# Layer norm before the experts' routing: half of the groups on ScalarE, and the first expert number read ahead

## The reference, cut to what matters

```python
x = x + retention(_layernorm(x))
x = x + _moe(_layernorm(x), Wg, bg, w1, w2)
x = x + recurrence(_layernorm(x))
x = x + _moe(_layernorm(x), Wg, bg, w1, w2)

def _layernorm(x, axis=-1, eps=1e-05):
    return (x - mean) / sqrt(var + eps)

def _moe(x, Wg, bg, w1, w2):
    logits = t @ Wg.T + bg                      # 4096 x 8
    topw, topi = top_k(softmax(logits), 2)
    # each token goes to its two experts:
    #   gate, up = split(t @ w1e.T); o = (silu(gate) * up) @ w2e.T
    # and the two results are added with normalised weights
```

## Time and profile before

| | us |
|---|---|
| median of 3 runs | 1347.71 |
| lowest and highest | 1342.36, 1349.99 |
| profiled execution, its own time | 1351.96 |
| its span, first to last instruction | 1350.1 |
| TensorE busy | 1148.6 (85%) |
| VectorE busy | 927.6 (69%) |
| ScalarE busy | 612.8 (45%) |
| GpSimd busy | 551.3 (41%) |

### The profile page before, as it was taken

One profiled execution on the slowest core, in us unless ns is written; L12 is line 12 of the kernel. 1 busy time (PEld: TensorE's weight loads), 2 busy tenths in 40 slices (PEclk: granted clock), 3 DMA queues, 4 the chain that ended last, 5 costly groups with the idle time before them and its releaser, 6 DMA issues. The chain is left out here.

```text
span 1350.1 us, 34954 instructions
## 1 busy us (share of the span) xinstructions
PE 1148.6 (85%) x14041; PEld 818.7 (61%) x14041; DVE 927.6 (69%) x1959; ACT 612.8 (45%) x1310; POOL 551.3 (41%) x537
## 2 busy tenths in 40 slices
PE   7999999975699999478999999899987648999970
PEld 4677777763588888235555555555555436888850
DVE  6778787757765655568778797877854376656546
ACT  3344343413355555153736456374653233555534
POOL 3333233202377776325162341516321105777750
PEclk9999999988799999698999999999997679999995
DMA  8132222009643332200000101000000195333338
GB/s 305 55 109 95 88 93 86 35 1 346 209 170 104 104 102 89 72 32 3 33 3 33 33 3 33 4 32 4 2 2 3 33 387 159 104 103 103 105 108 336
DMA packets 50682, 125.66 MB, mean 93 GB/s; under 512 B 7648, under 2 KB 26976, under 8 KB 47712
## 3 DMA queue, kind: packets, MB, share of 16 engines
q1 hardware_dynamic: 36896, 86.20, 17.8%
q0 software_dynamic: 13632, 37.24, 8.8%
HBM read 79.63 MB, written 43.78 MB: 91 GB/s over the span
## 5 line engine op out<-in xcount | busy, mean ns | idle before, releaser
L1090 POOL DMA_INDIRECT ffn_xs<-xn_rows,ffn_from_row x142 | 137.7, 969 | 123.0 <-DVE ffn_second_y_at L1472 80.4
L1098 POOL DMA_INDIRECT y_rows<-ffn_ys,ffn_to_row x142 | 140.2, 987 | 54.9 <-issue 35.2
L1253 PE MATMUL ffn_ps_h<-ffn_w_high,ffn_xst 128*128 x568 | 155.1, 395 | 0.7 <-issue 0.7
L1500 DVE TENSOR_TENSOR ffn_act_in<-ffn_silu_g,ffn_ps_h 128x256 f32<-128x256 f32 x142 | 59.9, 422 | 139.1 <-ACT ffn_silu_g L1132 139.1
L1132 ACT ACTIVATE ffn_silu_g<-ffn_ps_h 128x256 f32<-128x256 f32 x142 | 54.8, 386 | 144.3 <-PE ffn_ps_h L1253 144.3
L1273 PE MATMUL ffn_ps_o<-ffn_w,ffn_act_t 128*128 x284 | 117.2, 435 | 0.5 <-DVE ffn_act_t L1505 0.5
L1253 PEld LDWEIGHTS ffn_ps_h<-ffn_w_high,ffn_xst 128*128 128x128 f32 x568 | 97.3, 190 | 18.2 <-issue 1.2
L1833 POOL TENSOR_TENSOR rec_mixed_w<-rec_mixed_w,rec_xnt 128x512 f32<-128x512 f32 x16 | 17.2, 1090 | 200.0 <-DVE rec_mixed_w L2635 200.0
L1253 PE MATMUL ffn_ps_h<-ffn_w_low,ffn_xst 128*128 x284 | 89.8, 398 | 0.0
L644 DVE TENSOR_TENSOR ret_probs<-ret_score,ret_causal 128x2048 f32<-128x2048 f32 x32 | 73.3, 2292 | 18.2 <-PE ret_score L485 18.2
L1275 PE MATMUL ffn_ps_o<-ffn_w,ffn_act_t 128*128 x284 | 79.2, 279 | 0.0
(11 more groups left out here) (353 smaller groups left out, 2890.2 us busy)
## 6 DMA issues: line engine op xcount, KB each, us to landing
home<-y_rows SPq DMA_DIRECT2D x30, 512.0 KB, 4.8
w_split<-home SPq DMA_DIRECT2D x24, 512.0 KB, 4.3
ffn_w_high<-w_split SPq DMA_DIRECT2D x8, 1024.0 KB, 8.8
ffn_w_low<-w_split SPq DMA_DIRECT2D x8, 1024.0 KB, 10.6
ffn_w<-w_split SPq DMA_DIRECT2D x8, 1024.0 KB, 14.6
home<-in_f_w SPq DMA_DIRECT2D x12, 512.0 KB, 5.8
xn_rows<-home SPq DMA_DIRECT2D x12, 512.0 KB, 11.7
out<-x SPq DMA_DIRECT2D x8, 512.0 KB, 5.7
```

What stands on the lines that cost most here:

```text
L1090: pool.indirect_dma_start(xs[:, n % SLOTS, :], None, xn_rows[:], bass.IndirectOffsetOnAxis(ap=from_row[:, n:n + 1], axis=0)) \
L1098: pool.indirect_dma_start(y_rows[:], bass.IndirectOffsetOnAxis(ap=to_row[:, m:m + 1], axis=0), ys[:, m % SLOTS, :], None).then_inc(ys_stor ...
L1253: mm = pe.matmul(ps_h[:, u % 2, :], one_pass(xst[:, u % 2, part, k, :]), one_pass(w1[w_part][k][:, bass.ds(e, E_COLUMNS)]), start=(part + ...
L1500: dve.tensor_tensor(act_in[:, u % 2, :], silu_g[:, u % 2, :], ps_h[:, u % 2, FF:2 * FF], ALU.mult) \
```

## The change

Two edits. In the norm stage, VectorE norms the even groups as before. The odd groups (1, 3, 5, 7) are normed by ScalarE, as `Identity(x * rstd + offset)`, where `offset` = -mean * rstd is made by VectorE in four small operations, one for each piece of GpSimd's. On ScalarE, group 1 and group 3 come ahead of xnt(0), group 5 ahead of xnt(2), and group 7 ahead of xnt(4). The semaphore `xn_ready` becomes two, one for each engine. In the loop's start, the wait for w1 and the TENSOR_LOAD of the first packed expert numbers come ahead of the transposes of the first two row tiles. The other edits of the diff are a new name (`expert_at` for `offset`) in TensorE's code.

```diff
+        offset = sb("offset", [P, TILES])
...
-        xn_ready = sem("xn_ready")
+        ln_offset = sem("ln_offset")
+        xn_ready = [sem(f"xn_ready{h}") for h in range(2)]
...
-                    sp.wait_ge(xn_ready, n + 1)
+                    sp.wait_ge(xn_ready[n % 2], n // 2 + 1)
...
             @block.scalar
             def _(act):
+                def norm(n):
+                    act.wait_ge(ln_offset, sum(first <= n for first in ROOTS))
+                    for j in range(UNROLL):
+                        i = n * UNROLL + j
+                        op = act.activation(xn_of[n][:, j, :], x[:, i, :], ACT.Identity, bias=offset[:, i:i + 1],
+                                            scale=rstd[:, i:i + 1])
+                    op.then_inc(xn_ready[1], 1)
+
+                norm(1)
                 for n in range(STEPS):
+                    if n % 2 == 0 and n + 3 < STEPS:
+                        norm(n + 3)
                     act.wait_ge(xt_in_psum, n + 1)
...
                 def transpose_norm(n):
-                    pe.wait_ge(xn_ready, n + 1)
+                    pe.wait_ge(xn_ready[n % 2], n // 2 + 1)
...
                 pe.wait_ge(route_step, EXPERTS_OF)
+                pe.wait_ge(w1_loaded, 16 * len(first_loads))
+                expert_at = {0: expert(experts_at(0), LAG)}
                 transpose_x(0, 0)
                 transpose_x(1, 1)
-                pe.wait_ge(w1_loaded, 16 * len(first_loads))
-                offset = {0: expert(experts_at(0), LAG)}
-                hidden(0, 0, offset[0])
+                hidden(0, 0, expert_at[0])
...
                 for n in range(STEPS):
-                    dve.wait_ge(ln_rstd, sum(first <= n for first in ROOTS))
-                    for j in range(UNROLL):
+                    if n in ROOTS:
+                        part = slice(n * UNROLL, ROOTS[ROOTS.index(n) + 1] * UNROLL)
+                        dve.wait_ge(ln_rstd, sum(first <= n for first in ROOTS))
+                        dve.scalar_tensor_tensor(offset[:, part], mean[:, part], -1.0, rstd[:, part], ALU.mult, ALU.mult) \
+                            .then_inc(ln_offset, 1)
+                    for j in range(UNROLL if n % 2 == 0 else 0):
                         i = n * UNROLL + j
                         op = dve.tensor_scalar(xn_of[n][:, j, :], x[:, i, :], mean[:, i:i + 1], rstd[:, i:i + 1],
                                                ALU.subtract, ALU.mult)
-                    op.then_inc(xn_ready, 1)
+                    if n % 2 == 0:
+                        op.then_inc(xn_ready[0], 1)
```

More of the change, by code:

```diff
@@ L1298, in turn_of_loop @@
                         if n >= LAG:
-                            output(n - LAG, (n - LAG) % UNROLL, offset[n - LAG])
+                            output(n - LAG, (n - LAG) % UNROLL, expert_at[n - LAG])
                         if n + 1 < NTILES:
-                            offset[n + 1] = expert(packed, LAG + n % UNROLL + 1)
-                            hidden(n + 1, (n + 1) % UNROLL, offset[n + 1])
+                            expert_at[n + 1] = expert(packed, LAG + n % UNROLL + 1)
+                            hidden(n + 1, (n + 1) % UNROLL, expert_at[n + 1])
                     if turn == TURNS - 1:
@@ L1305, in turn_of_loop @@
                         for n in range(NTILES - LAG, NTILES):
-                            output(n, n % UNROLL, offset[n])
+                            output(n, n % UNROLL, expert_at[n])
                 pe.wait_ge(route_step, FROM_ROW)
```

## The result

The changed kernel is slower: 1362.41 us (median of 4 runs, 1360.94 to 1363.36) against 1348.85 (1342.36 to 1355.16), ratio 1.0086 with a 95% interval of 1.0055 to 1.0118, so about 11.6 us. The ratio is an estimate over the single executions and not the quotient of the two medians, which lie 13.6 us apart; in what follows, too, a ratio on record can differ from the quotient of the medians beside it. The forecast was 5.4 us more, 1353.1, in a range up to 1359.5. The sign held; the size was forecast less than half as large as it is, and the range ended too low.

The account below looks back on a forecast made before the run. The prediction took the norm stage to be bound by TensorE and ScalarE waiting on each other. ScalarE's groups add 5.8 us and the load takes off 0.4: 1347.7 + 5.4 = 1353.1 us, range 1346.0 to 1359.5.

Parts of the forecast that it names:

- The sign: Whole kernel: forecast slower, by 5.4 us on the median.
- What bounds the stage: Norm stage: TensorE's transposes and ScalarE's copies wait on each other; VectorE's norms are hidden, with 5.00 us idle behind them.
- The label on T(3): Norm stage: the transposes of group 3 show a wait for VectorE's norm line, though that group was normed 2.7 us earlier.
- Rival B: Norm stage: TensorE really waited for VectorE's norms, so the time falls by 2.6 us to 1345.1; chance 0.07.
- The price of a group on ScalarE: Norm stage: four activations norming one group occupy ScalarE 1.6 us, with bounds of 1.4 and 2.0.
- Where the groups lie: Norm stage: groups 1 and 3 cost 0, group 5 costs 1.4 and 1.2 us, group 7 costs 1.6 in each layer.
- the touch on xnt(0): Norm stage, second layer: at 2.0 us a group, groups 1 and 3 would delay ScalarE's first copy by 0.4 us.
- Rival A, the clock: Gate stage: longer pauses halve TensorE's clock, costing 3.5 us in one layer (1356.6) or both (1360); chance 0.14.
- Rival C, the clock that comes back more kindly: Loop's first product: full instead of half clock in both layers gives back 2.9 us, 1350.2; chance 0.13.
- The shift passes straight to the loop: Behind the norm stage: routing is a chain of VectorE, so the stage's delay reaches loop and end in full.
- Sum: 3.0 in the first layer, 2.8 in the second: Norm stage: ScalarE's groups delay both layers by 5.8 us together, bounds 5.0 and 7.8.
- The load: Loop's start: loading expert numbers ahead of the transposes saves 0.4 us in the first layer, 0 in the second.

Follow-up runs that it names:

- e7: The kernel of e4 with ScalarE's norms as Copy with a scale alone, the mean not subtracted; 1362.08 us, one execution.
- e2: The changed kernel with the load of the expert numbers put back behind the transposes; 1363.66 us, ratio 1.0093.
- e4: The changed kernel with the tile `offset` allocated behind `ys`, so the loop's tiles lie where they lay before; 1356.07 us, ratio 1.0033.
- e6: The changed kernel with `offset` allocated behind `ys` and only group 7 normed by ScalarE; 1352.76 us, one execution.
- e5: The changed kernel with `offset` allocated behind `ys` and only group 5 normed by ScalarE; 1346.84 us, one execution.
- e1: The kernel before with the 128-byte tile `offset` allocated behind `rstd` and never used; 1354.26 us against 1353.31, ratio 1.0026.
- e9: The kernel before with 256 unused bytes in each partition behind `rstd`; loops 174.3 and 174.6 us, one execution.
- e11: The kernel before with 128 unused bytes in each partition ahead of `xst`; loops 177.0 and 177.2 us, one execution.
- e3: The kernel before with only the load of the expert numbers moved ahead of the transposes; 1346.88 us, ratio 0.9962.
- e10: The kernel before with 64 unused bytes in each partition behind `rstd`; loops 176.1 and 176.3 us, one execution.

## Why the prediction was wrong

*What bounds the stage*: right. VectorE's norms were off the path; its wait grew from 5.00 to 13.71 us. The label on T(3) was a coincidence, as argued; in the changed kernel, with half of the norms gone, the same wait is put down to ScalarE. Rival B did not happen.

*The price of a group on ScalarE, "I take 1.6"*: the term that was mis-sized. It is 1.97. The row was right in size and memory but had no bias, and it ran another function; e7 shows that these two together are the difference, 0.49 a step against 0.40. The trace of the kernel before had the right row, and the prediction overlooked it: the recurrence norms its own tiles on ScalarE with the same function, size, memories, scale and bias, four in 2.06 us:

```profile
587.24 2.06 ACT L1909 ACTIVATE home<-x,rec_offset,rec_rstd 128x256 f32<-128x256 f32 x4
```

```profile
L1909 ACT ACTIVATE home<-x,rec_offset,rec_rstd x32: 584/587/600, 551.6 to 937.9; 128x256 f32<-128x256 f32 x32
```

That is 0.587 each and (2.06 - 0.587) / 3 = 0.49 a step, to the last digit what the changed kernel showed. I had discarded the row with the bias (L389) because halving its step gave 0.35. But a step has a part that does not shrink with the size: the two rows with a bias, 0.71 for 512 columns and 0.49 for 256, differ by 0.22, so half the columns take off 0.22 and not 0.35. The halving was wrong in kind. The Trainium skill's 2.05 ("ScalarE: Activation LUTs", Rules for kernel authors), which the prediction set aside, was nearer, and the trace agrees with it: 2.06 for four, of which 1.97 pass before the next copy starts. Its 0.51 for one, though, lies between the 0.587 of one and the 0.49 from start to start.

*Where the groups lie*: right. With 1.97, xnt(4) comes 3.6 us later in the first layer (18.7 behind the start in place of 15.1) and 3.9 in the second (18.3 in place of 14.4), 7.5 in all against bounds of 5.0 to 7.8, and 0.4 of the second is the touch on xnt(0) that the prediction named.

*Rival A, the clock*: it happened, in the changed kernel in the first layer alone, from T(6) on: T(6) started 3.6 us late and the logits came 4.9 late, so it cost 1.3 and not 3.5. Its chance of 0.14 was too low: behind the pause of 2.65 us T(6) ran at half the clock in the first layer of the changed kernel, of e2 and of e4, and at full in the second layer of all three; in e6 the clock fell in both layers. What decides between the layers is open.

*Rival C, the clock that comes back more kindly*: it happened too, in the first layer. The first four matmuls of the loop's first product took 1.20 us at a granted clock of 1.00, where before they took 2.07 at 0.50 (359.3 to 362.3):

```profile
363.66 1.20 PE L1266 MATMUL ffn_ps_h<-ffn_w_high,ffn_xst 128*128 x4
```

```profile
363.70:365.40 1.70, 1.70 (x9) 1.38 (x10) 0.42 (x1) 0.29 (x2) 1.09 (x3) 1.00 0.28 84
```

From the first product to the first silu it is 1.70 us in place of 2.96, so 1.3 came back, of the 2.9 that the rival had for both layers; in the second layer only 0.2 did (2.80 against 2.96). e2, e4 and e5 show the same, 1.7 in the first layer and 2.85 to 2.96 in the second, and e7 1.7 in both. So it is no accident of one execution, but what decides where the clock rises is open. With it the first layer adds up: logits 4.9 later, 0.2 in the routing, 0.5 off by the load and 1.3 by this, 3.3 at the loop's start. "The shift passes straight to the loop" was wrong by this too.

*The part that was not in the sum at all*: the tile. This is the step that failed before all others; the price of a group comes second (7.5 us of shift in the two layers in place of 5.8). "Sum: 3.0 in the first layer, 2.8 in the second" and "the shift passes straight to the loop and to the end" put the loops at nothing: they assume that a loop whose instructions are the same takes the same time. It took 2.9 and 3.4 us more, which alone exceeds what the profile shows beyond the forecast (9.6 against 5.4), and e1, e4, e9 and e11 tie it to 128 bytes ahead of `xst`. No rival named it. With the tile out of the way, in e4, the kernel lies 4.5 us over before (1.1 to 8.0), close to the forecast of 5.4; that closeness is in part luck, since the norm stage cost about 3 us more than forecast in e4 as well (logits 4.8 and 3.9 later) and the first products gave 1.4 back.

*The load*: from the cast's start to the first product it is 2.73 and 2.48 in the changed kernel against 3.21 and 2.72: -0.5 and -0.2, against -0.4 and 0. Right in size there, and the spread over all kernels (e3) says the same. But the kernel before gains more than that from the load alone, which the prediction did not foresee and the profile does not explain.

*The recurrence* took 4.0 us less in the changed kernel's profile. Over the fourteen profiles this stretch ranges from 531.6 to 541.7 us with no order by kernel (534.9 in e1, 541.7 in e2 and in e4), so nothing ties the -4.0 to the change, and it hid part of the loss in the profile: without it the stages add up to 13.6 us, against the 7.4 to 15.9 of the interval.

## What to carry to other kernels

Before work moves to an engine that looks idle, find the wait that ends last in that stage, and look for that engine's pauses in the timeline: the same group cost 2 us between two copies and nothing one position earlier, in the pause. A step's price is taken from a row with the same function and operands, bias included, and such a row is looked for in the whole trace, other layers too. A new tile is not free even when it is small: compare the period of the hottest loop with and without it, and allocate it behind the loop's tiles.

## What the runs showed of the hardware that had not been expected

- An unused 128 bytes in each partition ahead of the stationary operands lengthened the loop's first products (512 columns) from 392 to 398 ns and the loop's period from 2.506 to 2.554 us, 1.9%; 64 bytes gave 2.540, 256 bytes 2.509 (before, e1, e9, e10, e11).
- An activation of 128x256 f32 from SBUF to SBUF takes 0.09 us more as Identity with a scale and a bias for each partition than as Copy with the scale alone, in duration (0.494 to 0.587) and in step (0.40 to 0.49) (the changed kernel, e7, and L1173 and L1909 of the kernel before).
- After a pause of 2.65 us TensorE's next eight transposes ran at 2.4 GHz in some stretches (1.06 us) and at 1.2 GHz in others (1.94 us), of the same program and within one execution (the changed kernel, e2 and e4). Behind a pause of 2.28 us it was 1.94 in e7.
- The first product of the loop ran at a granted clock of 1.00 in the first layer of the changed kernel and at 0.50 in that of the kernel before, which moved the loop's start by 1.3 us.
